# One chunk in eight of the edge scaling is done by VectorE instead of GpSimd

## What is computed

```python
h_src = h[src]                                   # one row of 256 for each edge, 8 heads of 32
ex = jnp.exp(alpha - amax[dst])                  # one weight for each edge and head
denom = jax.ops.segment_sum(ex, dst, num_segments=n)
attn = ex / jnp.maximum(denom[dst], 1e-10)
out = jax.ops.segment_sum(h_src * attn[..., None], dst, num_segments=n)
```

## Time and profile before

| | us |
|---|---|
| median of 3 runs | 2626.3 (2623.33 to 2627.14) |
| the profiled execution, its own time | 2624.72 |
| its span, first to last instruction | 2622.9 |
| stage of weighted sums, GpSimd's first scaling to VectorE's last addition | 2378.6 to 2578.0 |
| granted TensorE clock, mean over the span | 0.815 of full speed |

### The profile page before, as it was taken

The page is one execution under the profiler, slowest core; times in us unless marked ns, Lnnn a source line. Parts: engine busy times, 40 slices in busy tenths (PEclk is TensorE's granted clock), DMA queues, the critical chain, the costliest instruction groups (busy, mean ns, idle before and its releaser), DMA issues.

```text
span 2622.9 us, 39941 instructions
## 1 busy us (share of the span) xinstructions
PE 2163.6 (82%) x9949; PEld 1371.4 (52%) x9950; DVE 1447.8 (55%) x4125; ACT 711.9 (27%) x1814; POOL 1628.7 (62%) x1354
## 2 busy tenths in 40 slices
PE   2558657999995999999999999998776776647993
PEld 2446545777773444444444444445554554436772
DVE  6979997888885001000000011125877777777888
ACT  3234322222221000000000000002333333329993
POOL 1288888888887444444444444203777777758995
PEclk8557656555555999999999999999988888878996
DMA  9832222222222655435544444543777777766993
GB/s 390 324 26 2 1 0 1 0 0 0 0 0 6 174 141 139 138 109 139 131 138 120 128 125 137 164 124 90 219 219 218 218 219 218 218 192 192 286 288 110
DMA packets 296724, 350.60 MB, mean 134 GB/s; under 512 B 104538, under 2 KB 223025, under 8 KB 294065
## 3 DMA queue, kind: packets, MB, share of 16 engines
q1 hardware_dynamic: 207553, 274.47, 33.7%
q0 software_dynamic: 89072, 74.97, 16.6%
HBM read 242.39 MB, written 106.86 MB: 133 GB/s over the span
## 4 chain that ended last, share of the span: by engine, by line
PE 46%; POOL 25%; issue 12%; DVE 9%; DMA 5%; ACT 1%; DVEq 1%; SPq 0%; ACTq 0%; POOLq 0%
PE psum L917 30%; POOL adjacency L601 14%; POOL gath L624 11%; PE psum L1034 7%; DVE found L1419 4%; DMA gath<-gat_rows,rec 3%; PE psum L668 2%; PE psum L906 2%; PE psum L914 1%; PE psum L862 1%; DMA ea_in<-in_edge_attr 1%; DMA adjacency<-total,place 1%; DVE acc L1817 0%; PE psum L848 0%; PE psum L854 0%
## 5 line engine op out<-in xcount | busy, mean ns | idle before, releaser
L601 POOL DMA_INDIRECT adjacency<-total,place x392 | 614.5, 1568 | 221.5 <-issue 114.6
L610 POOL DMA_INDIRECT rows_by_dst<-rec,place x392 | 376.3, 960 | 446.8 <-PE psum L917 422.7
L624 POOL DMA_INDIRECT gath<-gat_rows,rec x416 | 400.3, 962 | 263.0 <-DMA gat_rows<-s_src 136.5
L917 PE MATMUL psum<-a_t,acc 128*128 128x512 f32 x1200 | 527.7, 595 | 29.9 <-DMA a_t<-adjacency 29.9
L917 PEld LDWEIGHTS psum<-a_t,acc 128*128 128x128 f32 x1200 | 228.8, 191 | 300.9 <-issue 298.2
L917 PE MATMUL psum<-a_t,x 128*128 128x512 f32 x600 | 262.2, 592 | 0.0
L989 PE MATMUL psum<-x,acc 128*128 x832 | 257.0, 457 | 5.1 <-DVE acc L1647 5.1
L1419 DVE SCALAR_TENSOR_TENSOR found<-psum,key_f,not_before 128x128 bf16<-128x128 f32 (+6 forms) x392 | 247.3, 696 | 0.0
L820 PE MATMUL psum<-table,ohhiT 32*128 32x128 f32 x784 | 238.3, 456 | 0.7 <-ACT table L1127 0.3
L1588 DVE TENSOR_SCALAR et<-et 128x512 f32<-128x512 f32 (+1 forms) x28 | 11.7, 416 | 410.3 <-ACT et L1168 407.1
L989 PEld LDWEIGHTS psum<-x,acc 128*128 128x128 f32 x832 | 179.0, 229 | 50.0 <-issue 17.0
(11 more groups left out here) (298 smaller groups left out, 2983.5 us busy)
## 6 DMA issues: line engine op xcount, KB each, us to landing
a_t<-adjacency SPq DMA_DIRECT2D x450, 256.0 KB, 2.6
gat_h_by_edge<-gath SPq DMA_DIRECT2D x104, 528.0 KB, 4.1
gath<-gat_h_by_edge SPq DMA_DIRECT2D x104, 528.0 KB, 4.8
adjacency<-zeros SPq DMA_DIRECT2D x12, 2178.5 KB, 55.0
adjacency<-zeros POOLq DMA_DIRECT2D x6, 2178.5 KB, 26.1
gath<-gat_rows,rec POOLq DMA_INDIRECT x416
adjacency<-total,place POOLq DMA_INDIRECT x392, 3.0
rows_by_dst<-rec,place POOLq DMA_INDIRECT x392
```

Source lines behind the costliest of these rows:

```text
L601: pool.indirect_dma_start(out=adj, in_=total[:, c:c + 1], out_offset=bass.IndirectOffsetOnAxis(ap=place[:, 0, c:c + 1], axis=0), in_offset ...
L610: pool.indirect_dma_start(out=rows_dst, in_=rec[:, c, :], out_offset=bass.IndirectOffsetOnAxis(ap=place[:, 1, c:c + 1], axis=0), in_offset ...
L624: pool.indirect_dma_start(out=gath[:, g % 4, c % 4, :], out_offset=None, in_=hh_dram, in_offset=bass.IndirectOffsetOnAxis(ap=rec_i[:, c, 0 ...
L917: i = pe.matmul(sums[b], table_g[:, w, b * P:(b + 1) * P], a_t[:, q % NA, 0:width(g)], start=k == 0 and g < OWN_GROUPS and w == 0, stop=w ...
```

## The change

In the quads with odd g, GpSimd scales only chunks 0 to 2, and VectorE scales chunk 3, with an instruction of 128 x 256 values placed right behind the `exp_columns` of that quad. Only the second of the two counts `s_vx`. VectorE waits for the load of the quad first. SP, before it loads into a buffer with an odd number, waits for VectorE's use of it too. Even quads are left as they are.

```diff
@@ sync: loading the rows of quad g
             for g in range(4, NQ):
                 sp.wait_ge(s_val, g - 3)
+                if g % 2:
+                    sp.wait_ge(s_vx, g - 3)
                 load_kept(g)
@@ gpsimd: scale_rows
+                    n = 4 - q % 2
                     nc.gpsimd.tensor_tensor(
-                        val[:, q, :, 0:D].rearrange("p c (h d) -> p c h d", h=HEADS),
-                        gath[:, q, :, 0:HX].rearrange("p c (h d) -> p c h d", d=HW)[:, :, :, 0:HD],
-                        s_sb[:, bass.ds(4 * g, 4), :].unsqueeze(3).broadcast_to([P, 4, HEADS, HD]),
+                        val[:, q, 0:n, 0:D].rearrange("p c (h d) -> p c h d", h=HEADS),
+                        gath[:, q, 0:n, 0:HX].rearrange("p c (h d) -> p c h d", d=HW)[:, :, :, 0:HD],
+                        s_sb[:, bass.ds(4 * g, n), :].unsqueeze(3).broadcast_to([P, n, HEADS, HD]),
                         ALU.mult).then_inc(s_val, 1)
@@ vector: exp_columns
-                v.tensor_reduce(val[:, q, :, D:HX], s_sb[:, bass.ds(4 * g, 4), :].unsqueeze(3), X,
-                                ALU.max).then_inc(s_vx, 1)
+                i = v.tensor_reduce(val[:, q, :, D:HX], s_sb[:, bass.ds(4 * g, 4), :].unsqueeze(3), X, ALU.max)
+                if q % 2:
+                    dve.wait_ge(s_ld[q], 16 * (g // 4 + 1))
+                    i = v.tensor_tensor(
+                        val[:, q, 3, 0:D].rearrange("p (h d) -> p h d", h=HEADS),
+                        gath[:, q, 3, 0:HX].rearrange("p (h d) -> p h d", d=HW)[:, :, 0:HD],
+                        s_sb[:, 4 * g + 3, :].unsqueeze(2).broadcast_to([P, HEADS, HD]), ALU.mult)
+                i.then_inc(s_vx, 1)
```

## The result

The changed kernel takes 2652.9 us (2649.4 to 2654.7) beside 2624.8 (2622.1 to 2627.1) for the kernel before: 1.0108 times, with a 95% interval of 1.0096 to 1.0120. That is 28 us slower; 2658 was predicted. The profiled execution is 2653.34 us, with a span of 2651.6; that of before was 2624.72.

A forecast was written before the change was run, and what follows sets the result against it. GpSimd was taken as the bound, by 0.10 us a quad; after the change VectorE, waiting 0.87 a pair: 51 x (3.51 + 0.87) + 3.51 = 226.9 against 194.9, so 2626.3 + 32 = 2658 us, range 2634 to 2681.

The forecast's parts named there:

- What bounds the kernel: Weighted-sums stage: GpSimd bounds at 1.88 us a quad, TensorE 1.78, ScalarE 1.78, VectorE 1.76; at most 7 us to gain.
- The wait: VectorE's new two-SBUF-input instruction stands until GpSimd's running scaling ends, ending 0.28 behind it; main case, chance 0.81.
- The order at the end of a wait: When GpSimd's running scaling ends, VectorE's instruction takes its turn before GpSimd's queued one, as read off the divisions.
- W: VectorE's wait for GpSimd's scaling, once per pair of quads: taken as 0.87 us, kept between 0.45 and 1.25.
- The hop h: Delay from VectorE's addition 1 to TensorE's second matmul two quads on; no row shows it, taken as 0.13.
- the circle: Addition 1 delays TensorE, whose end releases GpSimd's long scaling, which sets VectorE's next wait: 0.74 plus the hop.
- The sum: Additions go from 194.9 us to 51 pairs x (3.51 + 0.87) + 3.51 = 226.9, or +32.0, giving 2658.
- SP's wait costs nothing: SP's new wait before loading is for VectorE work done a whole buffer turn before, so it costs nothing.
- No contention: Rival: VectorE's new instruction never waits for GpSimd; a pair costs 3.74 against 3.75 now, time 2626; chance 0.09.
- By the load: Rival: VectorE waits 1.2 for quad g + 3's load in each pair, +55 us, 2681; chance 0.04.
- By the order: Rival: GpSimd's queued instruction goes first, each wait grows by a short scaling, 1.48; some 2733; chance 0.03.
- As meant: Rival: the new instruction isn't felt and TensorE's 1.78 a quad holds throughout; -7 us, 2619; chance 0.03.

The follow-up runs named there:

- the smaller scaling alone: Changed kernel without VectorE's new instruction, its wait and SP's; chunk 3 of odd quads is set to 1 once and not computed: 2619.0 us, ratio 0.9987.
- one-input run: Changed kernel, but VectorE's new instruction reads one tensor: it copies chunk 3 and leaves the factor out; 2619.2 us, ratio 0.9991.
- the factor in PSUM: Changed kernel, VectorE's weights copied once to unused PSUM columns and read there: 2624.2 us for each odd quad, 2622.0 with VectorE scaling in each fourth only.
- the added instruction alone: Changed kernel, but GpSimd scales all four chunks and VectorE also does its new instruction, into an unread scratch tile: 2633.3 us, ratio 1.0050.
- three-ahead run: Changed kernel, but GpSimd may be three quads ahead of TensorE, not four: 2637.5 us, ratio 1.0056.
- the run without the tie: Changed kernel, VectorE's instruction in its own place reading a resident tile, without its load wait and SP's wait for VectorE: 2650.5 us, ratio 1.0096.
- the runs behind addition 1: Changed kernel, new instruction moved behind addition 1 of the quad: 2645.2 us; the same reading a resident tile, without load wait and SP's wait: 2645.7 us.
- both runs without the tie behind an addition: Changed kernel, new instruction reading a resident tile, without load wait and SP's wait, moved behind addition 1 (2645.7 us) or addition 2 (2637.7 us).

## Why the prediction was right

*What bounds the kernel.* GpSimd by 0.10 a quad, the rest close behind, 7 us to gain at most. The run with the smaller scaling alone shows 3.4 by the runs and 5.2 by its profile. Right for GpSimd; but the 7 took TensorE's pace to be the next bound, and it is VectorE's 1.755 with the losses that the prediction knew of, 3.63 a pair against TensorE's 3.56.

*The wait.* That VectorE's instruction stands until the running scaling ends, ends itself 0.28 and goes on 0.20 behind it, was read off the divisions and holds to the hundredth. The one-input run and the factor in PSUM show that it is all of the loss.

*The order at the end of a wait.* VectorE goes before GpSimd's queued instruction: in no pair of the changed kernel does it wait for two; with GpSimd's next scaling queued up, the run with the added instruction alone shows it directly (2.10 in place of 1.91).

*The size of W.* 0.87 was predicted for the wait and 3.51 for the rest of a pair; measured are 1.00 and 3.39 (2463.92 to 2464.92 of 4.39). Two terms were off, by 0.13 and by 0.12 in opposite ways, and cancelled in the sum: that 4.38 came out as 4.39 is luck, the mechanism isn't. The rest is shorter, presumably as VectorE's queue goes on with the register work while the instruction waits, and the additions behind it follow at 0.34, not 0.365 (2465.12 to 2466.14). And the wait is longer, as VectorE asks that much sooner, and as TensorE's end comes later: from its restart at 2465.59 to GpSimd's start at 2467.39 are 1.80, where 1.71 had been summed. The hop h from an addition to TensorE, unknown before, is 0.05. The three-ahead run shows that W is a phase: moving the release by one quad brings the other scaling across the request, at the place and with the length reckoned.

*The sum.* 51 pairs at 4.38 were to add 32; they added 31.0 in the profile. The pairs took 4.39 where the circle was closed, but the first twelve quads took 24.3, where six such pairs take 26.3; the circle closed with the wait in quad 12, probably since VectorE has to fall behind by two quads first. The rest took 201.6, where 200.6 was summed. From 2658 to 2653, 1.5 are the lower median of before in these runs; in the profiled execution the stage's earlier start makes 2.3.

*SP's wait costs nothing.* Right for the time, and wrong in its reason. VectorE does not do its part "a whole buffer turn before": two quads behind TensorE, it reads an odd quad's rows after GpSimd has scaled them, and the load goes out on its signal. In the changed kernel the load still lands in time (the run without the tie is no faster); in the runs behind addition 1 and with the factor in PSUM it doesn't always, though without the tie the run behind addition 1 took as long (23 us over the kernel before in both).

*The rivals.* No contention: excluded by the rows, of which only 4 of 52 take 0.41 to 0.43 and 44 take over 1.2. By the load: VectorE waited for a load once, 0.3 us. By the order: excluded. As meant: excluded.

## What to carry to other kernels

Work moved from GpSimd to VectorE doesn't run beside it if VectorE reads both operands from SBUF and GpSimd's instruction reads SBUF too: in this kernel VectorE's instruction stands for the rest of the running one, and the price is set by how much of that is left when VectorE asks (0.1 to 1.9 us here), not by its own 0.41. An operand in PSUM or an instruction of one input makes the wait vanish (1.27 to 0.41 us here). When such a wait is in a loop, find which engine is the bound first: with GpSimd as the bound the same instruction cost 11 us (2633.3 against 2621.9), with GpSimd relieved 28. And count the pace of the engine that takes the work over, its regular losses included: without any wait, VectorE's own 3.74 a pair used up all that relieving GpSimd gave.

## What was not expected of the hardware

- Relieving GpSimd of a quarter of each second scaling, with VectorE's instruction in place, made the kernel slower by 17 us (from 11 to 28 over the kernel before), and a stricter wait of GpSimd made it faster by 12 (16 over it).
- The additions behind an instruction that waited for GpSimd follow at 0.34 for a quad, where 0.36 to 0.37 is the rule without a wait. It fits that VectorE's queue goes on with the register work meanwhile; no run tests that.
- A small loss, repeated, sets off large waits: VectorE stands 0.35 once in six quads, at fixed places of its written-out code (quads 52, 58, 64, 70, 76 and 82 in both runs without the tie behind an addition). Where the margin between its request and the end of a scaling is smaller than that, each loss costs a wait for a whole scaling more: a row of 1.55 in each third pair (behind addition 2), of 1.7 (behind addition 1, second half). What the loss itself is, no run shows.
